# A mixture-of-experts layer: shared units at other expert steps, a count behind the last scatter, more additions ahead

## What is computed

```python
logits = xt @ gate_w.T + gate_b                     # 8 experts
top_w, top_i = jax.lax.top_k(softmax(logits), 2)     # two experts for each token
def expert(w1e, b1e, w3e, b3e, w2e, b2e):            # hidden width 128
    h = silu(xt @ w1e.T + b1e) * (xt @ w3e.T + b3e)
    return h @ w2e.T + b2e
y = sum of the two chosen experts' results, each by its weight
z = silu(xt @ ws1.T + bs1) * (xt @ ws3.T + bs3) @ ws2.T + bs2   # shared expert, width 256
x = x + tanh(g_ffn) * (y + z)
```

## Time and profile before

| what | us |
|---|---|
| median of three runs | 737.16 |
| the three runs | 731.80, 737.64, 737.16 |
| the profiled execution | 731.16 |
| its span from first to last instruction | 729.4 |
| PE, DVE, ACT, POOL busy | 553.3, 425.1, 321.4, 323.5 |
| TensorE clock granted over the span | 0.848 |

### The profile page before, as it was taken

One profiled execution on the slowest core, in us unless ns is written; L12 is line 12 of the kernel. 1 busy time (PEld: TensorE's weight loads), 2 busy tenths in 40 slices (PEclk: granted clock), 3 DMA queues, 4 the chain that ended last, 5 costly groups with the idle time before them and its releaser, 6 DMA issues.

```text
span 729.4 us, 22147 instructions
## 1 busy us (share of the span) xinstructions
PE 553.3 (76%) x8750; PEld 453.9 (62%) x8750; DVE 425.1 (58%) x1369; ACT 321.4 (44%) x777; POOL 323.5 (44%) x446
## 2 busy tenths in 40 slices
PE   5889777777777786787777778788798788797930
PEld 3667566666666664665555566677677677676830
DVE  5678745754756645556565656554554554554658
ACT  3677634644646444634444333243443343343410
POOL 1122335344344455334445463346456466455540
PEclk9999978967989878856775757999999999999875
DMA  4313113113223222222211126855455455551199
GB/s 151 100 57 109 59 49 99 61 50 102 59 62 93 71 77 72 75 56 71 71 46 42 32 94 198 277 165 167 129 166 166 129 172 155 149 161 62 40 367 357
DMA packets 60936, 84.21 MB, mean 115 GB/s; under 512 B 11056, under 2 KB 36656, under 8 KB 60688
## 3 DMA queue, kind: packets, MB, share of 16 engines
q1 hardware_dynamic: 49232, 59.31, 27.0%
q0 software_dynamic: 8640, 17.84, 7.2%
q10 hardware_dynamic: 2960, 5.62, 2.1%
HBM read 52.33 MB, written 24.02 MB: 105 GB/s over the span
## 4 chain that ended last, share of the span: by engine, by line
PE 31%; DVE 17%; issue 17%; ACT 13%; another core or an unknown queue 12%; POOL 5%; DMA 2%; SPq 1%; DVEq 0%; ACTq 0%; POOLq 0%
PE BANKS L538 4%; ACT PT L815 4%; PE BANKS L528 4%; PE BANKS L652 3%; ACT YW L939 3%; PE BANKS L513 3%; POOL RS L1299 2%; ACT SG L943 2%; PE BANKS L657 2%; DVE ST L984 2%; PE BANKS L781 2%; PE BANKS L772 2%; PE BANKS L782 2%; PE BANKS L575 2%
## 5 line engine op out<-in xcount | busy, mean ns | idle before, releaser
L1351 POOL DMA_INDIRECT expert_results<-YW,XB x142 | 136.7, 963 | 124.2 <-ACT YW L939 82.1
L1282 POOL DMA_INDIRECT routed_rows<-STAGED,IDX x128 | 126.1, 985 | 47.1 <-issue 38.4
L528 PE MATMUL BANKS<-CST,LATE 128*128 128x128 f32 x512 | 80.5, 302 | 33.8 <-issue 29.7
L815 ACT ACTIVATE PT<-BANKS 128x512 f32<-128x512 f32 x128 | 71.8, 612 | 62.6 <-remote 47.3
L1293 POOL TENSOR_TENSOR VE<-MV,EPSV 128x4 f32<-128x4 f32 (+1 forms) x35 | 6.9, 197 | 205.7 <-DVE MV L988 205.6
L538 PE MATMUL BANKS<-VX,PT 128*32 128x18 f32 x4096 | 69.4, 203 | 34.2 <-issue 30.5
L528 PEld LDWEIGHTS BANKS<-CST,LATE 128*128 128x128 f32 x512 | 63.3, 155 | 51.4 <-issue 44.2
L939 ACT ACTIVATE YW<-YB,XB 128x128 f32<-128x128 f32 x142 | 48.9, 392 | 98.5 <-DVE YB L1233 75.3
L538 PEld LDWEIGHTS BANKS<-VX,PT 128*32 128x32 f32 x4096 | 57.9, 131 | 46.8 <-issue 41.8
L993 DVE TENSOR_REDUCE MX<-BANKS 128x16 f32<-128x1024 f32 x32 | 39.1, 1222 | 60.5 <-remote 45.5
L815 ACT ACTIVATE VX<-BANKS 64x128 f32<-64x128 f32 x128 | 35.2, 275 | 87.0 <-PE BANKS L565 83.1
(11 more groups left out here) (145 smaller groups left out, 1095.7 us busy)
## 6 DMA issues: line engine op xcount, KB each, us to landing
LATE<-in_experts SPq DMA_DIRECT2D x71, 257.0 KB
XB<-routed_rows SPq DMA_DIRECT2D x71, 130.0 KB
XCT<-in_inputs_t SPq DMA_DIRECT2D x32, 256.0 KB
X<-in_x SPq DMA_DIRECT2D x32, 128.0 KB
out<-X ACTq DMA_DIRECT2D x16, 256.0 KB, 4.8
LATE<-QK SPq DMA_DIRECT2D x126, 32.0 KB, 2.3
X2T<-expert_results SPq DMA_DIRECT2D x13, 256.0 KB
STAGED<-expert_results SPq DMA_DIRECT2D x12, 256.0 KB, 8.9
```

The lines of the kernel that those rows point to most:

```text
L528: last = nc.tensor.transpose(T[half][:, o:o + 128], cols, ident)
L815: return nc.scalar.activation(dst, src, ACT.Copy)
L1282: nc.gpsimd.indirect_dma_start(routed[:, :], bass.IndirectOffsetOnAxis(ap=IDX[:, s, g.slots.start + t:g.slots.start + t + 1], axis=0), STA ...
L1351: nc.gpsimd.indirect_dma_start(results[:, :], bass.IndirectOffsetOnAxis(ap=XB[:, b, p, a, DIM + 1:DIM + 2].bitcast(i32), axis=0), YW[:, b ...
```

## The change

Three edits. The table of the steps without a shared unit is another one: after steps 0 and 1 every fifth step (6, 11, ..., 26) instead of every fourth (5, 9, ..., 29), and the last two steps, 34 and 35. The count of step 34 stands behind the last scatter of step 35 instead of ahead of it. And the final part of DVE runs four first-result additions before its loop, which adds one more at each turn, instead of one. Line numbers behind the edits are two to three higher than before.

```diff
-UNSHARED = (0, 1, 5, 9, 13, 17, 21, 25, 29)
+UNSHARED = (0, 1, 6, 11, 16, 21, 26, 34, 35)
...
+ADDED_AHEAD = 4
...
-                add_first(0)
+                for n in range(ADDED_AHEAD):
+                    add_first(n)
                 for n in range(CSTEPS):
-                    if n + 1 < CSTEPS:
-                        add_first(n + 1)
+                    if n + ADDED_AHEAD < CSTEPS:
+                        add_first(n + ADDED_AHEAD)
...
-                            if n >= 1 and (p, a) == (parts(n)[-1], 0):
+                            if 1 <= n < STEPS - 1 and (p, a) == (parts(n)[-1], 0):
                                 note_sent(n - 1)
...
-                note_sent(STEPS - 1)
+                for n in (STEPS - 2, STEPS - 1):
+                    note_sent(n)
```

## The result

The change made the kernel a little slower: over 22 runs of each the changed kernel's median is 741.18 us, that of the kernel before 735.37; the ratio is 1.0072 with a 95% interval from 1.0043 to 1.0101, so +5.3 us. (The medians are of all 22 runs; the ratio leaves out runs more than 1.5% above the fastest of their kernel, so it is not quite the quotient of the medians.) The forecast was +0.5 us. The time, 741.18, lies within the stated range of 727 to 742, near its upper end, and the change is within 1%; but the loss is clear of noise and ten times what was forecast.

A forecast was written before the change was run, and what follows sets the result against it. No engine was taken as full: lateness fills the expert steps, then full DMA engines and DVE's additions set the ending. Terms +1.6 + 0 - 1.1 gave +0.5 us; added to 734.4, the forecast was 735.0 us, range 727 to 742.

The forecast's parts named there:

- The price of a unit ahead of step 32: Expert steps before step 32: each of two added shared units costs 0.80 us, read from two step pairs; together +1.6 us.
- the upper bound: PE's own time for one shared unit, 2.78 us; two cost +5.6 us where the cover of idle time is gone.
- What hides the other 2 us of each unit is PE's idle time.: Expert steps: PE's idle time, 8.2 us per eight steps, covers the rest of each added unit's work.
- PE becomes the bound: Rival, chance 0.16: in steps 27 to 33 lateness adds to PE's work; +4.5 us (735.7), at half clock +10.0 (741.2).
- The units of steps 34 and 35 are worth nothing there.: After step 32: removing the two units from the last steps gains nothing, since nothing on the path waits for those tiles.
- The count behind the last scatter, 0.: Steps 34 and 35 on POOL: last scatter issued 4 to 8 us sooner, but only the last load needs it; worth 0.
- Four additions ahead, -1.1 us.: Final additions on DVE: three more move into 2.83 us of idle time; DVE's count gives -1.8, -1.1 us taken.
- My slack of 1.1 us behind 724: Ending: DMA engines fall to 292 and 303 GB/s after 724 us, leaving 1.1 us that stores asked for earlier can use.
- The sum.: Whole kernel: +1.6 + 0 - 1.1 = +0.5 us, the profiled execution going from 731.16 to 731.7 us; chance 0.50.
- four rivals: Transfers alone set the end (0.12), PE becomes the bound (0.16), late places move (0.18), nothing visible (0.02).
- The late places.: Rival, chance 0.18: bare steps meet the 2 to 4 us delays on even steps and shrink them; 725.7 down to 719.7 us.

The follow-up runs named there:

- The seven comparisons: Whole change twice, table alone twice, old spacing with two more units ahead, three more ahead, two left out, each against the kernel before: ratios 0.9945 to 1.0119.
- the three comparisons at 571 and 572 us: Against the kernel before: the table alone 1.0049, the whole change again 1.0052, old spacing with two more units ahead of step 32 1.0091.
- the earlier trace: Profile of the kernel before, from which the prediction was made: span 729.4 us, profiled execution 731.16 us.
- three more units: Table (0, 1, 6, 12, 18, 24, 33, 34, 35) alone, three more shared units ahead of step 33 than the kernel before: 1.0119 at 753 us.
- the first pair: The first profiles of the kernel before and of the whole change: spans 729.4 and 737.1 us.
- two units left out: Every third step bare, shared units 30 and 31 not computed, two units fewer ahead of step 32 than the kernel before: 0.9945 at 753 us.

## Why the prediction was wrong, point by point

*The price of a unit ahead of step 32 (forecast 0.80 us, +1.6 for two).* This step failed. The 0.80, taken as "read in the very rhythm that the change continues", came from two pairs of steps that differ by lateness as much as by work. The seven comparisons gave 1.4 to 3.0 us a unit where 0.80 was forecast; the table alone measured +2.8 and +3.8 us for two. PE's own time for it, in the undisturbed stretches, is 2.1 to 2.2 us (the three comparisons at 571 and 572 us gave 1.4, 1.5 and 2.6); the upper bound that I had from the earlier trace rows, 2.78, was the nearer row.

*"What hides the other 2 us of each unit is PE's idle time."* This is the reason behind the failed number, and it is wrong: further units did not fit into PE's idle time. At 753 us PE had 33 us of idle time in 24 steps and three more units still cost 9.0 us. The rival "PE becomes the bound" had the mechanism that the profiles at 571 us show, but I tied it to growing lateness; there it needs none. Its lowest price, 5.6 us for two, is above all that two units measured. For the slower chips, where the prediction was made, the price is shown and the mechanism is not.

*The units of steps 34 and 35 are worth nothing there.* Right, measured at 571 us only: 1.0018 with them left out.

*The count behind the last scatter, 0.* The step held: the wait is gone and the last scatter comes 9.3 us after the first load instead of 16.4 (710.38 - 701.04, against the earlier trace rows). The count was never tried without the additions, so its 0 rests on the two together showing nothing.

*Four additions ahead, -1.1 us.* The row of additions shrank by 1.8 us, as counted. But the end took most of it back, 4.1 us of stores instead of 2.7 in the first pair, and nothing is left in the ratios. The term was mis-sized: the two parts together gave 0.4 us in the first pair and 0.03 us between two profiles at 753 us. My slack of 1.1 us behind 724 was to a large part not free capacity. The rule of the Trainium skill that I weighed (DMA: Bandwidth & Descriptors, Issuing engines are not separate DMA queues) is that all issuers' transfers interleave on the same 16 DMA engines. By it the term was 0, and the runs came near that, with the engines 1.05 busy.

*The sum.* With 2.2 us for each unit and 0 for the additions, the steps of the forecast give +4.4 us; the whole change measured +5.3 and +3.0. (The chances of the forecast and its four rivals add up to 0.98, a slip.) That the time fell into the range is owed to its width, made for the spread of the runs, and not to the sum.

*The late places.* They did not move in the change's favour. In the first pair, the stretch from step 2's copy to step 33's took 212.65 us before and 213.10 after, and the loss came behind it: step 33's own time was 6.35 us and is 8.76. That one execution puts the loss at a late place by the end, and step 32's copy to the first load does not follow the number of units: 21.9 us again in the table alone at 732 us, but also 21.4 in a kernel with the old table and 22.7 with two units left out, at 753 us. That the loss over many runs belongs to the two units rests on the ratios.

*What stays open.* What makes the releases late at 732 to 753 us and not at 571, and with it how a unit comes to cost its full time there. In the profile at 753 us ACT waits 34 us for releases that nothing explains in 24 steps, in the one at 571 us for none; the program is the same, the chip another. I have no experiment on it. Also open is why moving units ahead of the steps does not pay.

## What to carry to other kernels

Do not count an engine's idle time as cover for new work until you know what the engine waits for: here PE had 33 us of it and added units still cost their full time. Ask of a unit of work not only on which engine it stands but on which side of the point that starts the next part: here two units were free behind the point at which the transfers start, and cost some 2 us each ahead of it. And a shorter row of instructions in front of full DMA engines need not end the kernel sooner: 1.8 us less of additions gave 0.4 us at most.

## What the runs showed of the hardware that I had not expected

The same program took 571 and 572 us on two chips and 732 and 753 on two others, with the same busy time of DVE (424.7 us at 571, 425.1 in the first profile) and less of PE (483.0 against 553.3); the granted clock over the span was 0.942 and 0.848. It is not a matter of the expert steps alone: step 0's copy stands at 353.6 us at 571 and at 459.6 in the first profile, so 106 us of the difference are attention's. At 571 us the expert steps keep PE 100% busy at full clock, at 753 us PE is busy 142.91 of 176.30 us at a clock of 0.94.

In that slower condition releases from PE seem to come late, and not by a fixed delay. In the waits of 24 steps at 753 us (who waited for whom, total us, times, longest) one row has no counterpart at 571 us:

```profile
ACT SGS L917 <- remote: 34.0, 6, 6.4
```

Six waits of up to 6.4 us, each ending 3.6 to 5.3 us after the recorded end of the PE matmuls that ACT needed. One of them, on PE and on ACT:

```profile
578.10 1.03 PE L575 MATMUL BANKS<-X2T,SW 128*128 128x256 f32 x4
...
582.72 0.84 ACT L917 ACTIVATE SGS<-BANKS,SW 128x256 f32<-128x256 f32 x2 [5.50 <-remote]
```

The ends of matmuls are modelled in the profile, so it cannot tell a late release from an end recorded too early. The number of these waits does not follow the table: between step 5 and step 29 the old table had 6, 6 and 11 of them in three profiles, the new one 5 and 6, three more units ahead 9. At 571 us the same activation waits for PE by name, at most 1.0 us:

```profile
ACT SGS L917 <- PE BANKS L575: 17.1, 18, 1.0
```
